# Sums of weight blocks moved from VectorE to GpSimd, with planning steps, loads and copies reordered and matmuls put between two stages

## Chip, cores, metric

One of the cores of a Trainium2 chip runs the whole program. The metric is the device time of one execution in microseconds; lower is better.

## What is computed

x is 32 batches of 64 rows and 1024 columns. Four layers are applied, each added to its input:

```python
# W0, W1: (16, 64, 64), picked per batch by itok_B_0_15
x = x + einsum('bct,bcd->bdt', x, W0[c])
x = x + einsum('bct,bcd->bdt', x, W1[c])
# W: (1024, 1024); lora_A: (5, 1024, 32); lora_B_w: (1024, 32)
x = x + einsum('bsi,oi->bso', x, W) + einsum('bsr,or->bso', einsum('bsi,bir->bsr', x, A[l]), B) * 0.5
# weight: (8, 1024, 1024), picked per batch by itok_B_3_7
x = x + einsum('bsi,boi->bso', x, weight[a])
```

## The kernel before

The two small layers act on the 64 rows and the two large ones on the 1024 columns, so the kernel does the large ones first on x transposed and applies the product of the two small ones (`mix_tab`, 16 matrices of 64x64) at the end. To each large weight the identity is added on its diagonal (`w_eyes`, L451; `A11`, L1088; `adapter_eyes`, L421), which gives the residual.

**Precision.** Every float32 operand is split into a high part (a copy to float32r by ACT: `w_hi`, `x_hi`) and a low part (source minus high part, by DVE: `w_lo`, `x_lo`). A product is then three matmuls, high by high, high by low, low by high (L1288 to L1290, in `main`). The semaphores `w_hi`, `x_hi`, `w_lo`, `x_lo` count tiles, four to a block.

**Layer 3 (W) as seven products.** W and x are cut in 2x2 blocks and multiplied by a Strassen scheme: seven weight blocks (w 0 to 6) and sixteen x blocks (x 0 to 15, twice seven and two), in two column groups j = 0 and 1. Some operands are sums of raw blocks. For the weights: S2 = `kw + w1t - w2t`, in `kw`; S3 = `w2t - w1t`, in `w2t`; S1 = w5's block + S2; S4 = w6's block - S2. For x: T1 to T4. Before, DVE forms all of them: `s2_and_s3` (L892, L894, L896), `s1` (L902), `s4` (L908), `t1` to `t4`. Each works on 128 partitions by 2048 columns.

**The low-rank part** is `low_rank(c, ...)` (L1315, 32 matmuls of 256 columns), done four times: the second one, `low_rank(1, 1, 3)`, waits for `x_lo` to reach 16, which is all of x block 3; the third, `low_rank(2, 11, 12)`, for all of x12. ACT and DVE then fold the result (`low_out`: L550, L555; `low_parts`: L922, L926), and a matmul adds it (L1327).

**Layer 4** is done slot by slot (two batches with the same adapter at a time; L1402, and L1429 for the mix with `mix_tab`). Which batches share a slot is worked out on the chip by `plan_steps`, a chain of about a hundred small DVE operations on 32 partitions, each waiting for the one before. It is a generator that yields after every few operations; `take(n)` emits the next n pieces at a place in DVE's order where there is room: `take(2)` ahead of `s2_and_s3`, `take(4)`, and a last `take()` with all the rest.

**Order.** Nothing is scheduled by a planner: each engine runs its instructions in the order in which its block is written, and waits on semaphores. The SP queue issues nearly all loads, in its own order, with waits of its own. PE starts with `warm(WARM)` (20 matmuls on zeroes), makes `mix_tab` (16 products of 64 columns, L1267, after DVE has made `w1_s` and `w0_twice` at L822 and L826), and goes on to the first product of layer 3.

Of the kernel before, what the change touches and what calls it, by code (L numbers as in the profile page):

```python
# [13 lines left out]
P = 128  # L14
# [14 lines left out]
RING = 12  # L29
UNIT = 2 * D  # L30
HALF = KT // 2
WARM = 20


BATCH0, BATCH1, SINGLE = (0, 5), (5, 5), (10, 1)
# [31 lines left out]
def build(nc, xt, indices, w0t, w1, wt, lora_a, lora_b, w3t, plan_c, eye_c, out):  # L67
# [120 lines left out]
    def s(name):  # L188
        if name not in sem:
            sem[name] = nc.alloc_semaphore(name)  # L190
        return sem[name]
# [56 lines left out]
    with nc.Block() as block:  # L248
# [3 lines left out]
        def _(sp):  # L252
# [5 lines left out]
            def load_x(n, half, c):  # L258
                if n >= 3:
                    wait_l2(sp, x_last[n - 3])  # L260
                sp.dma_start(raw_of(x_slot(n)), x_block(half, c)).then_inc(s(f"x_in{n}"), 16)

            def load_w(w, out_half, in_half):
                if w >= 3:
                    wait_l2(sp, w_last[w_before(w)])
                sp.dma_start(raw_of(w_slot(w)), w_block(out_half, in_half)).then_inc(s(f"w_in{w}"), 16)

            def load_stg(half, c):
                sp.dma_start(stg, x_block(half, c)).then_inc(s("stg"), 16)
# [39 lines left out]
            load_stg(1, 0)  # L309
            load_w(5, 1, 1)  # L310
            load_x(10, 1, 2)
            load_x(11, 1, 2)
            sp.wait_ge(s("T1"), 1)
            load_stg(2, 2)
            load_w(6, 1, 2)
            sp.wait_ge(s("S4"), 1)
            load_kw(x_block(1, 3))
# [91 lines left out]
        def _(pool):  # L409
# [38 lines left out]
            def w_eyes(dst, name):  # L448
                for k in range(HALF):
                    v = dst[:, k, P * k:P * (k + 1)]  # L450
                    pool.tensor_tensor(v, v, eye[:, 0:P], ALU.add).then_inc(s(name), 1)  # L451

            pool.wait_ge(s("S3"), 1)
            w_eyes(w2t, "S3")
            pool.wait_ge(s("w_in4"), 16)
            w_eyes(raw_of(w_slot(4)), "A22")
            pool.wait_ge(s("S1"), 1)
            w_eyes(raw_of(w_slot(5)), "S1")


            pool.wait_ge(s("low_lo"), 2 * CH)
# [39 lines left out]
        def _(act):  # L501
# [25 lines left out]
            def x_from(n, src, name, value):  # L527
                act.wait_ge(s(name), value)
                if src is not None:

                    wait_l2(act, x_last[n - 3])
                for ks in halves:
                    x_hi(n, raw_of(x_slot(n)) if src is None else src, ks)
# [36 lines left out]
            def c21(j, os=range(HALF)):  # L570

                act.wait_ge(s("seed"), HALF * (j + 1))
                copy_out("C21", 1, j, out_block(2, j), "c21", os)
# [9 lines left out]
            def w_from(w, src, name, value):  # L583
                act.wait_ge(s(name), value)
                if w >= 3 and src is not None:

                    wait_l2(act, w_last[w_before(w)])
                for ks in halves:
                    w_hi(w, raw_of(w_slot(w)) if src is None else src, ks)
# [43 lines left out]
            x_from(5, keep, "T3", 1)  # L633
            c11(1, last_two)
            w_from(3, w2t, "S3", HALF + 1)
            u2(0)
            x_from(6, None, "T4", 1)
            w_from(4, None, "A22", HALF)
            u3(0, first_two)
            for pair in range(8, 12):  # L640
# [7 lines left out]
            c21(0, last_two)  # L648

            act.wait_ge(s("x_lo"), HALF * 9)  # L650
            u2(1)
            x_from(9, None, "T4", 2)
            u3(1)
            w_from(5, None, "S1", HALF + 1)
            x_from(10, None, "T1", 1)
            c21(1, first_two)
            x_loaded(11)
            c21(1, (2,))
            x_from(12, stg, "stg", in_stg("B22_0"))
            c21(1, (3,))  # L660
            w_from(6, None, "S4", 1)
            low_out(2)
            for pair in range(12, 16):
                select(pair)
            x_from(13, kw, "T1", 2)
# [150 lines left out]
        def _(dve):  # L816
# [4 lines left out]
            v = w1_s.rearrange("p (c n) -> p c n", n=T)  # L821
            dve.tensor_tensor(v, v, eye[:, P:P + T].unsqueeze(1).to_broadcast([P, half, T]), ALU.add).then_inc(s("w01i"), 1)  # L822
            dve.wait_ge(s("w0"), 16)
            v = w0_s.rearrange("p (c n) -> p c n", n=T)
            for cs in (slice(0, half // 2), slice(half // 2, half)):
                dve.tensor_tensor(w0_twice[:, cs], v[:, cs].unsqueeze(2).to_broadcast([P, half // 2, 2, T]),  # L826
                                  eye[:, P:P + T].unsqueeze(1).unsqueeze(1).to_broadcast([P, half // 2, 2, T]), ALU.add)\
                   .then_inc(s("w01i"), 1)

            def w_lo(w, src, ks=slice(0, HALF)):  # L830
                dve.wait_ge(s("w_hi"), HALF * w + ks.stop)
# [13 lines left out]
            def w_los(w, src):  # L845
                for ks in halves:
                    w_lo(w, src, ks)

            def x_los(n, src=None):
                for ks in halves:  # L850
                    x_lo(n, src, ks)
# [24 lines left out]
            def t1(j):  # L876

                dve.wait_ge(s("stg"), in_stg(f"B11_{j} again"))
                if j == 0:
                    dve.wait_ge(s("x_in10"), 16)  # L880
                    v = raw_of(x_slot(10))
                else:
                    dve.wait_ge(s("kw"), 48)
                    v = kw
                dve.tensor_tensor(v, v, stg, ALU.subtract).then_inc(s("T1"), 1)

            def s2_and_s3():

                dve.wait_ge(s("w1t"), 16)
                dve.wait_ge(s("w2t"), 16)  # L890
                dve.wait_ge(s("kw"), 32)
                dve.tensor_tensor(kw, kw, w1t, ALU.add).then_inc(s("S2"), 1)  # L892
                dve.wait_ge(s("S2"), 1)
                dve.tensor_tensor(kw, kw, w2t, ALU.subtract).then_inc(s("S2"), 1)  # L894
                dve.wait_ge(s("S2"), 2)
                dve.tensor_tensor(w2t, w2t, w1t, ALU.subtract).then_inc(s("S3"), 1)  # L896

            def s1():

                dve.wait_ge(s("w_in5"), 16)  # L900
                v = raw_of(w_slot(5))
                dve.tensor_tensor(v, v, kw, ALU.add).then_inc(s("S1"), 1)  # L902

            def s4():

                dve.wait_ge(s("w_in6"), 16)
                v = raw_of(w_slot(6))
                dve.tensor_tensor(v, v, kw, ALU.subtract).then_inc(s("S4"), 1)  # L908

            def add_out(event, phase, j, src, dst, name, os=range(HALF)):  # L910
                for o in os:
# [166 lines left out]
            def take(n=None):  # L1078
                for _ in itertools.islice(making, n):
                    pass  # L1080
# [24 lines left out]
                                         ALU.mult, ALU.subtract).then_inc(s("b_split"), 1)  # L1105
            low_parts(0)
            dve.wait_ge(s("consts"), 32)
            take(2)
            s2_and_s3()
            x_los(3)  # L1110
            t3(0)
            t2(0)
# [2 lines left out]
            x_los(4, stg)  # L1115
            x_los(5, keep)
            w_los(3, w2t)
            take(4)
            t4(0)
            x_los(6)  # L1120
            w_los(4, raw_of(w_slot(4)))
# [4 lines left out]
            take()  # L1126
            t4(1)
            x_los(9)
            s1()
            t1(0)  # L1130
            w_los(5, raw_of(w_slot(5)))
            x_los(10)
            x_los(11)
            x_los(12, stg)
            s4()
            low_parts(2)
            w_los(6, raw_of(w_slot(6)))
            c22(0)
# [114 lines left out]
        def _(pe):  # L1253
# [6 lines left out]

            warm(WARM)

            for c in range(NC_ // 2):
                pe.wait_ge(s("w01i"), 2 if c < NC_ // 4 else 3)
                for g in range(2):
                    rows = slice(g * T, (g + 1) * T)
                    last = pe.matmul(ps_low[:, g, T * c:T * (c + 1)],  # L1267
                                     w0_twice[rows, c, :, :].rearrange("p h n -> p (h n)"),
                                     w1_s[rows, T * c:T * (c + 1)], start=True, stop=True)
            last.then_inc(s("mm"), 2)  # L1270

            def place_free(phase, j, o):
                n = HALF * (2 * phase + j) + o - NB
# [252 lines left out]
```

## Time and profile before

| | us |
|---|---|
| median of 3 runs | 394.65 |
| lowest, highest | 394.63, 395.87 |
| the profiled execution | 395.87 |
| its span | 394.1 |
| PE busy | 377.9 (96%) |
| DVE busy | 268.9 (68%) |
| ACT busy | 231.2 (59%) |
| POOL busy | 123.2 (31%) |

The span is what lies between the first and the last instruction of the profile. Times in the rows count from its start. A row of the timeline merges neighbouring instructions of one line; x2 behind it says that there are two. In square brackets stands the idle time of the engine before it and what ended it.

### The profile page before, as it was taken

To read this page: it belongs to the slowest core of one execution; us is meant where nothing else is said; L and a number is where in the kernel's file an instruction comes from. 1 tells how busy PE (TensorE), PEld (TensorE's weight loads), DVE (VectorE), ACT (ScalarE), POOL (GpSimd) and SP (SyncE) were. 2 spreads that over 40 slices of the span, in tenths; PEclk is the share of its full clock that TensorE was granted. 3 is DMA by queue.
4 is the path that set the end of the run, shared out by engine and by line. 5 is a ranking of instruction groups with operands and counts; after the bars stand their busy time and mean duration, and the time that the engine had idled before them with its cause. 6 is when DMAs were issued, how large, how long until landed. Compare 5 with 4: busy or idle time off the path is not lost.

```text
span 394.1 us, 7604 instructions
## 1 busy us (share of the span) xinstructions
PE 377.9 (96%) x1736; PEld 313.9 (80%) x1736; DVE 268.9 (68%) x285; ACT 231.2 (59%) x307; POOL 123.2 (31%) x163
## 2 busy tenths in 40 slices
PE   7989999999999999999999999899999999999981
PEld 6868888888888888888888887688888888888860
DVE  4766947864864968547968439953699446899562
ACT  3697849396332866244484549554677358777361
POOL 0000430100003000024864427753257434377400
PEclk9998999999999999999999999999999999999996
DMA  7985902741338565506518224742276322871223
GB/s 224 397 310 197 337 0 59 264 151 62 106 137 294 210 237 200 169 36 214 177 50 260 58 55 127 262 124 55 56 241 211 93 53 60 264 220 52 57 57 88
DMA packets 24219, 61.37 MB, mean 156 GB/s; under 512 B 1938, under 2 KB 2066, under 8 KB 24146
## 3 DMA queue, kind: packets, MB, share of 16 engines
q1 hardware_dynamic: 23808, 60.30, 46.3%
q8 instruction: 28, 0.46, 0.5%
q14 instruction: 45, 0.37, 0.3%
q10 hardware_dynamic: 338, 0.24, 0.2%
HBM read 52.15 MB, written 8.39 MB: 154 GB/s over the span
## 4 chain that ended last, share of the span: by engine, by line
PE 93%; issue 2%; DVE 1%; DMA 1%; ACT 1%; SPq 0%; ACTq 0%; DVEq 0%
PE ps L1402 44%; PE ps L1288 13%; PE ps L1290 13%; PE ps L1289 13%; PE ps L1315 4%; PE ps L1429 4%; PE ps L1327 2%; DMA ring_f<-wt 1%; DVE stage L1238 0%; DVE stage L1179 0%; PE ps L1448 0%; ACT stage L708 0%; DVE aT L1216 0%; DVE ring L833 0%; ACT ring L510 0%
## 5 line engine op out<-in xcount | busy, mean ns | idle before, releaser
L1402 PE MATMUL ps<-ring,aT 128*128 x784 | 180.8, 389 | 0.0
L1402 PEld LDWEIGHTS ps<-ring,aT 128*128 128x128 f32 x784 | 147.0, 188 | 30.9 <-issue 0.6
L1288 PE MATMUL ps<-ring 128*128 128x512 f32 x224 | 87.3, 390 | 1.2 <-DVE ring L840 1.2
L1289 PE MATMUL ps<-ring 128*128 128x512 f32 x224 | 87.2, 389 | 0.0
L1290 PE MATMUL ps<-ring 128*128 128x512 f32 x224 | 87.2, 389 | 0.0
L429 POOL TENSOR_TENSOR aT<-xT,aT 128x512 fp32r<-128x512 f32 (+1 forms) x36 | 55.9, 1574 | 48.5 <-ACT aT L687 43.4
L1151 DVE TENSOR_TENSOR ring<-raw,ring 128x1024 f32 (+1 forms) x40 | 64.4, 1668 | 5.1 <-ACT ring L673 5.0
L696 ACT ACTIVATE aT<-ps 64x1024 fp32r<-64x1024 f32 x32 | 32.7, 1023 | 47.5 <-PE ps L1402 47.0
L1168 DVE TENSOR_TENSOR aT<-ps,aT 64x1024 fp32r<-64x1024 f32 x32 | 39.1, 1222 | 22.6 <-ACT aT L696 21.9
L1179 DVE TENSOR_TENSOR stage<-ps,stage 64x1024 f32<-64x1024 f32 x30 | 36.7, 1222 | 26.0 <-ACT stage L708 25.3
L1288 PEld LDWEIGHTS ps<-ring 128*128 128x128 f32 x224 | 42.1, 188 | 9.9 <-DVE ring L833 1.3
L1290 PEld LDWEIGHTS ps<-ring 128*128 128x128 f32 x224 | 42.0, 188 | 8.7
L1289 PEld LDWEIGHTS ps<-ring 128*128 128x128 f32 x224 | 42.1, 188 | 8.6
L708 ACT ACTIVATE stage<-ps 64x1024 f32<-64x1024 f32 x30 | 30.6, 1018 | 23.8 <-PE ps L1429 23.4
L673 ACT ACTIVATE ring<-raw 128x1024 f32 (+1 forms) x40 | 39.6, 1049 | 8.0 <-POOL raw L421 5.6
L562 ACT ACTIVATE xT<-ps 128x512 f32<-128x512 f32 x40 | 22.6, 591 | 21.9 <-PE ps L1290 20.7
L421 POOL TENSOR_TENSOR raw<-raw,eye 128x128 f32<-128x128 f32 x40 | 20.6, 525 | 27.3 <-DMA raw<-w3t 23.2
L451 POOL TENSOR_TENSOR ring_f<-ring_f,eye 128x128 f32<-128x128 f32 x8 | 5.5, 718 | 68.9 <-DVE ring_f L902 50.6
L840 DVE TENSOR_TENSOR ring<-ring_f,ring 128x1024 fp32r<-128x1024 f32 (+1 forms) x20 | 21.9, 1127 | 5.6 <-ACT ring L513 5.5
L443 POOL CAST st<-aT 128x64 fp32r x34 | 19.1, 562 | 10.2 <-POOL st L445 7.6
L687 ACT ACTIVATE aT<-xT 128x512 fp32r (+1 forms) x36 | 19.9, 602 | 3.1 <-DVE xT L913 2.7
L451 POOL TENSOR_TENSOR xT<-xT,eye 128x128 f32<-128x128 f32 x4 | 7.7, 1942 | 43.7 <-DVE xT L896 43.7
(82 smaller groups left out, 312.0 us busy)
## 6 DMA issues: line engine op xcount, KB each, us to landing
raw<-w3t SPq DMA_DIRECT2D x40, 512.0 KB, 4.4
ring_f<-xt SPq DMA_DIRECT2D x8, 1024.0 KB, 8.2
raw<-xt SPq DMA_DIRECT2D x8, 1024.0 KB, 5.1
out<-stage SPq DMA_DIRECT2D x30, 256.0 KB, 3.0
ring_f<-wt SPq DMA_DIRECT2D x4, 1024.0 KB, 7.3
xT<-xt SPq DMA_DIRECT2D x3, 1024.0 KB, 9.5
xT<-wt SPq DMA_DIRECT2D x2, 1024.0 KB, 14.8
ring_f<-wt SPq DMA_DIRECT2D x4, 256.0 KB, 5.6
```

What stands on the lines that cost most here:

```text
L429: pool.tensor_tensor(x3_split(i, ks, P + h * T, T), xT[:, ks, bass.ds(which[h] * T, T)], as_f32(x3_split(i, ks, h * T, T)), ALU.subtract). ...
L562: act.activation(dst[:, o, :], ps_l2(phase, j, o), ACT.Copy).then_inc(s(name), 1)
L673: act.activation(dst, adapter_raw(t), ACT.Copy).then_inc(s("w_hi"), 1)
L696: act.activation(r_tile(h)[own, :], acc(i)[own, :, :].rearrange("p a n -> p (a n)"), ACT.Copy)\
L708: act.activation(stage[own, i % 2, :], mixed_ps[h][other, :, :].rearrange("p a n -> p (a n)"), ACT.Copy)\
L1151: dve.tensor_tensor(in_two(unit_of(t, 1)), adapter_raw(t), as_f32(in_two(unit_of(t, 0))), ALU.subtract)\
L1168: dve.tensor_tensor(r_tile(h)[other, :], acc(i)[own, :, :].rearrange("p a n -> p (a n)"), as_f32(r_tile(h)[own, :]), ALU.subtract).then_in ...
L1179: dve.tensor_tensor(dst, mixed_ps[h][own, :, :].rearrange("p a n -> p (a n)"), dst, ALU.add)\
L1288: pe.matmul(dst, hi_of(qw)[:, k, cs], hi_of(qx)[:, k, :], start=start and k == 0, stop=False, skip_group_check=True)
L1289: pe.matmul(dst, hi_of(qw)[:, k, cs], lo_of(qx)[:, k, :], start=False, stop=False, skip_group_check=True)
L1290: last = pe.matmul(dst, lo_of(qw)[:, k, cs], hi_of(qx)[:, k, :], start=False, stop=stop and k == HALF - 1, skip_group_check=True)
L1402: last = pe.matmul(acc(i)[:, n, :], x3_split(i, k, start, P), ring[:, bass.ds(off + (part * D + n * 512), 512)], start=(k == 0 and j == 0) ...
```

## The change

- **PE**: `mix_tab`'s sixteen products run over all eight column blocks of one half of the partitions and then of the other, and wait once; 20 more matmuls on zeroes (`BRIDGE`) stand between them and the first product of layer 3.
- **DVE**: `w0_twice` in one operation of 1024 columns instead of two; S2, S3, S1 and S4 leave DVE; `take(7)` instead of `take(2)` ahead of x block 3, and `take(2)` instead of `take(4)` ahead of T4; x10 is split ahead of w5.
- **POOL**: forms S2, S3, S1 and S4, each ahead of the diagonal that goes on it.
- **ACT**: x6 and x9 are copied one tile of `u2` earlier; x10 ahead of w5; `low_out(2)` ahead of w6.
- **SP**: the load of x11 stands behind the wait for T1 and the load of B22_0 to `stg`.

```diff
-WARM = 20
+WARM, BRIDGE = 20, 20
...
-            load_x(11, 1, 2)
             sp.wait_ge(s("T1"), 1)
             load_stg(2, 2)
+            load_x(11, 1, 2)
...
+            pool.wait_ge(s("w1t"), 16)
+            pool.wait_ge(s("w2t"), 16)
+            pool.wait_ge(s("kw"), 32)
+            pool.tensor_tensor(kw, kw, w1t, ALU.add).then_inc(s("S2"), 1)
+            pool.wait_ge(s("S2"), 1)
+            pool.tensor_tensor(kw, kw, w2t, ALU.subtract).then_inc(s("S2"), 1)
+            pool.wait_ge(s("S2"), 2)
+            pool.tensor_tensor(w2t, w2t, w1t, ALU.subtract).then_inc(s("S3"), 1)
             pool.wait_ge(s("S3"), 1)
             w_eyes(w2t, "S3")
             pool.wait_ge(s("w_in4"), 16)
             w_eyes(raw_of(w_slot(4)), "A22")
+
+            pool.wait_ge(s("w_in5"), 16)
+            v = raw_of(w_slot(5))
+            pool.tensor_tensor(v, v, kw, ALU.add).then_inc(s("S1"), 1)
             pool.wait_ge(s("S1"), 1)
-            w_eyes(raw_of(w_slot(5)), "S1")
+            w_eyes(v, "S1")
+            pool.wait_ge(s("w_in6"), 16)
+            v = raw_of(w_slot(6))
+            pool.tensor_tensor(v, v, kw, ALU.subtract).then_inc(s("S4"), 1)
...
-            u2(0)
+            u2(0, first_two)
+            u2(0, (2,))
             x_from(6, None, "T4", 1)
+            u2(0, (3,))
...
-            u2(1)
+            u2(1, first_two)
+            u2(1, (2,))
             x_from(9, None, "T4", 2)
+            u2(1, (3,))
             u3(1)
+            x_from(10, None, "T1", 1)
             w_from(5, None, "S1", HALF + 1)
-            x_from(10, None, "T1", 1)
...
+            low_out(2)
             w_from(6, None, "S4", 1)
-            low_out(2)
...
-            for cs in (slice(0, half // 2), slice(half // 2, half)):
-                dve.tensor_tensor(w0_twice[:, cs], ...).then_inc(s("w01i"), 1)
+            dve.tensor_tensor(w0_twice, ...).then_inc(s("w01i"), 1)
...
-            take(2)
-            s2_and_s3()
+            take(7)
             x_los(3)
...
-            take(4)
+            take(2)
             t4(0)
...
-            s1()
             t1(0)
+            x_los(10)
             w_los(5, raw_of(w_slot(5)))
-            x_los(10)
             x_los(11)
             x_los(12, stg)
-            s4()
...
-            for c in range(NC_ // 2):
-                pe.wait_ge(s("w01i"), 2 if c < NC_ // 4 else 3)
-                for g in range(2):
+            pe.wait_ge(s("w01i"), 2)
+            for g in range(2):
+                for c in range(NC_ // 2):
                     last = pe.matmul(...)
-            last.then_inc(s("mm"), 2)
+                last.then_inc(s("mm"), 1)
+            warm(BRIDGE)
```

DVE before, from the first planning steps to T3: `cells` holds the planning's values, `raw` is `kw` (or `stg`), `xT` holds `w1t`, `w2t` and `keep`.

```order
L963 CAST cells<-asked 32x32 [waits chain,consts]
L947 TENSOR_TENSOR cells<-cells,eye 32x32 [waits chain]
L959 TENSOR_REDUCE cells<-cells 32x1 [waits chain]
L947 TENSOR_TENSOR cells<-cells 32x256 [waits chain]
L959 TENSOR_REDUCE cells<-cells 32x8 [waits chain]
L892 TENSOR_TENSOR raw<-raw,xT 128x2048 [waits kw,w2t,w1t]
L894 TENSOR_TENSOR raw<-raw,xT 128x2048 [waits S2]
L896 TENSOR_TENSOR xT<-xT 128x4x512 [waits S2]
L840 TENSOR_TENSOR ring<-ring_f,ring 128x1024 [waits x_hi] x2
L857 TENSOR_TENSOR xT<-xT,raw 128x4x512 [waits stg,keep]
```

DVE in the change, the end of the same stretch (lines of the changed kernel, in which L858 is the split of x that was L840, and L875 is T3); ahead of these rows stand the same five planning steps and 15 more rows of planning:

```order
L958 COPY cells<-cells 32x32 [waits chain]
L962 STREAM_TRANSPOSE cells<-cells 32x32 [waits chain]
L950 SCALAR_TENSOR_TENSOR cells<-cells 32x32 [waits chain]
L954 TENSOR_REDUCE cells<-cells 32x1 [waits chain]
L950 SCALAR_TENSOR_TENSOR cells<-cells 32x32 [waits chain]
L954 TENSOR_REDUCE cells<-cells 32x1 [waits chain]
L946 TENSOR_SCALAR cells<-cells 32x32 [waits chain]
L954 TENSOR_REDUCE cells<-cells 32x1 [waits chain]
L858 TENSOR_TENSOR ring<-ring_f,ring 128x1024 [waits x_hi] x2
L875 TENSOR_TENSOR xT<-xT,raw 128x4x512 [waits stg,keep]
```

The three operations on 2048 columns are gone from here, and 25 planning operations have taken their place ahead of the split.

POOL before, between the first and the second clearing of `st`:

```order
L410 MEMSET st 128x512
L451 ISA
L451 TENSOR_TENSOR xT<-xT,eye 128x128 [waits S3,eye,zeroed]
L451 TENSOR_TENSOR xT<-xT,eye 128x128 x3
L451 TENSOR_TENSOR ring_f<-ring_f,eye 128x128 [waits w_in4]
L451 TENSOR_TENSOR ring_f<-ring_f,eye 128x128 x3
L451 TENSOR_TENSOR ring_f<-ring_f,eye 128x128 [waits S1]
L451 TENSOR_TENSOR ring_f<-ring_f,eye 128x128 x3
L463 MEMSET st 128x512 [waits low_hi,low_lo]
```

POOL in the change, the same stretch without its first two and its last row:

```order
L457 TENSOR_TENSOR raw<-raw,xT 128x2048 [waits w2t,w1t,kw,eye,zeroed]
L459 TENSOR_TENSOR raw<-raw,xT 128x2048 [waits S2]
L461 TENSOR_TENSOR xT<-xT 128x4x512 [waits S2]
L451 TENSOR_TENSOR xT<-xT,eye 128x128 [waits S3]
L451 TENSOR_TENSOR xT<-xT,eye 128x128 x3
L451 TENSOR_TENSOR ring_f<-ring_f,eye 128x128 [waits w_in4]
L451 TENSOR_TENSOR ring_f<-ring_f,eye 128x128 x3
L469 TENSOR_TENSOR ring_f<-ring_f,raw 128x2048 [waits w_in5]
L451 TENSOR_TENSOR ring_f<-ring_f,eye 128x128 [waits S1]
L451 TENSOR_TENSOR ring_f<-ring_f,eye 128x128 x3
L474 TENSOR_TENSOR ring_f<-ring_f,raw 128x2048 [waits w_in6]
```

Five operations on 2048 columns have come, the first three one behind the other.

ACT before, around w6 and `low_out(2)`; the last row of L513 is x12, L510 the two halves of w6:

```order
L513 ACTIVATE ring<-raw 128x1024 [waits l2,stg]
L513 ACTIVATE ring<-raw 128x1024
L562 ACTIVATE xT<-ps 128x512 [waits l2,seed]
L510 ACTIVATE ring<-ring_f 128x1024 [waits S4]
L510 ACTIVATE ring<-ring_f 128x1024
L550 ACTIVATE low<-ps 128x512 [waits l2]
L555 ACTIVATE low_split<-low 64x4x64 [waits l2,low_sum]
```

In the change the two rows of L510 stand behind all of `low_out(2)` (L550 and five of L555).

## Rows read from the trace of the kernel before

**Rows 1.** The page, busy time of the engines

```profile
PE 377.9 (96%) x1736; PEld 313.9 (80%) x1736; DVE 268.9 (68%) x285; ACT 231.2 (59%) x307; POOL 123.2 (31%) x163
```

**Rows 2.** PE's waits: who waited for whom, us in total, times, longest

```profile
PE ps L1448 <- DVE aT L1216: 3.3, 1, 3.3
PE ps L1315 <- issue: 2.0, 1, 2.0
```

**Rows 3.** The chain that ended last, in order of time: start, us, what

```profile
25.37 1.97 issue
27.34 5.55 PE ps L1315 x32
...
50.15 3.83 PE ps L1315 x32
...
138.33 3.83 PE ps L1315 x32
```

**Rows 4.** PE by stretch: length, PE busy (count), granted clock, DMA share, GB/s

```profile
27.00:28.00 1.00, 0.66 (x5) 1.00 0.46 170
28.00:29.00 1.00, 1.00 (x9) 0.70 0.09 35
29.00:30.00 1.00, 1.00 (x6) 0.50 0.00 0
```

**Rows 5.** DVE's timeline, 34 to 48 us: start, us, engine line operation

```profile
35.63 0.17 DVE L963 CAST cells<-asked 32x32 f32<-32x32 int32 x1
...
37.91 2.29 DVE L892 TENSOR_TENSOR raw<-raw,xT 128x2048 f32<-128x2048 f32 x1 [0.79 <-DMA raw<-wt]
...
44.77 2.62 DVE L840 TENSOR_TENSOR ring<-ring_f,ring 128x1024 fp32r<-128x1024 f32 x2
```

**Rows 6.** DVE's timeline, planning operations at 70 and 101 us

```profile
70.49 0.35 DVE L951 TENSOR_SCALAR cells<-cells 32x8 int32<-32x8 f32 x2
...
75.21 0.20 DVE L967 STREAM_TRANSPOSE cells<-cells 32x32 f32<-32x32 f32 x1
...
100.58 0.23 DVE L955 SCALAR_TENSOR_TENSOR cells<-cells 32x32 f32<-32x32 f32 x1
...
102.30 0.17 DVE L959 TENSOR_REDUCE cells<-cells 32x1 f32<-32x32 f32 x1
```

**Rows 7.** Timeline of POOL and DVE, single operations at 203 and 71 us

```profile
203.03 1.30 POOL L429 TENSOR_TENSOR aT<-xT,aT 128x512 fp32r<-128x512 f32 x1 [0.82 <-POOL st L445]
203.05 2.36 DVE L1151 TENSOR_TENSOR ring<-raw,ring 128x1024 f32 x1 [0.84 <-ACT ring L673]
204.28 2.28 POOL L429 TENSOR_TENSOR aT<-xT,aT 128x512 fp32r<-128x512 f32 x1
71.07 0.38 DVE L951 TENSOR_SCALAR cells<-cells 32x8 f32<-32x8 f32 x1
```

**Rows 8.** POOL's timeline, operations with nothing of DVE in the way

```profile
70.97 0.46 POOL L451 TENSOR_TENSOR ring_f<-ring_f,eye 128x128 f32<-128x128 f32 x1 [18.30 <-DMA ring_f<-wt]
216.78 2.55 POOL L429 TENSOR_TENSOR aT<-xT,aT 128x512 fp32r<-128x512 f32 x2 [1.29 <-issue]
```

**Rows 9.** Timeline of PE and DVE, 1 to 9 us

```profile
1.35 4.03 PE L1259 MATMUL ps<-st 128*128 128x256 f32 x20 [1.35 <-POOL st L410]
...
4.79 1.29 DVE L826 TENSOR_TENSOR stage<-stage,eye 128x512 f32<-128x512 f32 x2
...
5.54 2.00 PE L1267 MATMUL ps<-stage 64*128 64x64 f32 x32 [0.16 <-DVE stage L826]
...
8.77 0.47 PE L1288 MATMUL ps<-ring 128*128 128x512 f32 x1 [1.23 <-DVE ring L840]
```

**Rows 10.** Timeline of DVE, ACT and PE, 135 to 149 us

```profile
135.46 2.36 DVE L840 TENSOR_TENSOR ring<-raw,ring 128x1024 fp32r<-128x1024 f32 x2
140.11 2.01 ACT L510 ACTIVATE ring<-ring_f 128x1024 fp32r<-128x1024 f32 x2 [3.32 <-DVE ring_f L908]
143.55 2.18 ACT L555 ACTIVATE low_split<-low 64x256 fp32r<-64x256 f32 x5 [0.76 <-DVE low L922]
147.18 0.68 DVE L913 TENSOR_TENSOR xT<-ps,xT 128x512 f32<-128x512 f32 x1
148.37 0.39 PE L1288 MATMUL ps<-ring 128*128 128x512 f32 x1
```

More of the change, by code:

```diff
@@ L823, in _ @@
             dve.wait_ge(s("w0"), 16)
-            v = w0_s.rearrange("p (c n) -> p c n", n=T)
-            for cs in (slice(0, half // 2), slice(half // 2, half)):
-                dve.tensor_tensor(w0_twice[:, cs], v[:, cs].unsqueeze(2).to_broadcast([P, half // 2, 2, T]),
-                                  eye[:, P:P + T].unsqueeze(1).unsqueeze(1).to_broadcast([P, half // 2, 2, T]), ALU.add)\
-                   .then_inc(s("w01i"), 1)
+            dve.tensor_tensor(w0_twice, w0_s.rearrange("p (c n) -> p c n", n=T).unsqueeze(2).to_broadcast([P, half, 2, T]),
+                              eye[:, P:P + T].unsqueeze(1).unsqueeze(1).to_broadcast([P, half, 2, T]), ALU.add)\
+               .then_inc(s("w01i"), 1)
             def w_lo(w, src, ks=slice(0, HALF)):
@@ L885, in t1 @@
                 dve.tensor_tensor(v, v, stg, ALU.subtract).then_inc(s("T1"), 1)
[L887 to L908, printed above, removed]
             def add_out(event, phase, j, src, dst, name, os=range(HALF)):
@@ L1261, in _ @@
             warm(WARM)
-            for c in range(NC_ // 2):
-                pe.wait_ge(s("w01i"), 2 if c < NC_ // 4 else 3)
-                for g in range(2):
-                    rows = slice(g * T, (g + 1) * T)
+            pe.wait_ge(s("w01i"), 2)
+            for g in range(2):
+                rows = slice(g * T, (g + 1) * T)
+                for c in range(NC_ // 2):
                     last = pe.matmul(ps_low[:, g, T * c:T * (c + 1)],
```

## The prediction

> **What bounds the kernel now.** I read the page's list of busy time first: TensorE (PE) is at work for 377.9 of the 394.1 us [rows 1], so only what stops it or slows its clock counts. The list of PE's waits comes second [rows 2]: the one at the tail (3.3 us, before L1448) is not touched by the change; the one of 2.0 us before L1315, the first low-rank product, is. The chain in order of time [rows 3] places it: PE stops at 25.37, starts L1315 at 27.34, takes 5.55 us for its 32 matmuls, and from there shows no idle time up to the second low-rank product at 50.15, where the same 32 matmuls take 3.83. The difference, 1.7 us, is the clock: the granted clock stands at 0.50 of full, 1.2 instead of 2.4 GHz, from about 28.3 to 31.6, after the stop [rows 4]. The third low-rank product starts at 138.33 [rows 3]. The gain within reach at the front is therefore 2.0 + 1.7 us; what can be lost is whatever VectorE (DVE), ScalarE (ACT) or GpSimd (POOL) delivers late. The second low-rank product waits for all four low tiles of x block 3 (`x_lo` 16); DVE makes them in the two L840 that end at 47.39 [rows 5], 2.8 us before PE wants them at 50.15.
>
> **The front of PE.** w0_twice in one step ends at the same time as both halves did (4.79 + 1.29 = 6.08), so the sixteen small products start at 6.1 rather than 5.54 [rows 9]. They took 2.0 us; twenty bridge matmuls of 256 columns follow, at 0.12 us each (3.83 / 32, rows 3) 2.4 us. The main products start at 6.1 + 2.0 + 2.4 = 10.5 instead of 8.77: 1.7 late. From both sides: if the small products, now all of one half of the rows before the other, take twice as long (4.0) and the bridge runs like the warm-up (4.03), 14.1, that is 5.3 late. Taking the first, because the warm-up has ended its slow part by then, the 1.97 us stop shrinks to 0.2, L1315 starts at 27.3 as before, at full clock, and PE is ready for the second low-rank product at 50.15 - 1.7 = 48.4.
>
> **S2 and S3 move to POOL, and planning steps move ahead of x block 3.** This is the term that decides. On DVE, before: five planning operations from 35.63, three operations of 2.29 us from 37.91 (when `kw` has landed), then the split of x block 3 from 44.77 [rows 5]. After: thirty planning operations, then the split; the three big ones run on POOL meanwhile.
>
> Alone, the 25 added operations cost about what left: 19 of them ran from 70.49 to 75.41 and six from 100.58 to 102.47 [rows 6], together 4.9 + 1.9 = 6.8 us against 6.9. What changes the sum is that POOL and DVE hold each other up. At 203 us [rows 7] POOL's first L429 takes 1.30, the DVE operation issued beside it takes 2.36 where two of that size take 2.36 together elsewhere [rows 10], and POOL's next takes 2.28: each waits for the whole of the other's operation and then they take turns. It holds for the small planning operations as well: the first one beside a POOL operation of 0.46 takes 0.38 [rows 7], where two took 0.35 just before [rows 6]. The Trainium skill (SBUF — State Buffer, "SBUF: two separate sides") says the port pair that the two share is locked for a whole instruction; the trace agrees up to 512 columns, and no row has a longer POOL operation. By a lock let go within it, the rival below applies.
>
> Price of one POOL operation on 2048 columns: 0.46 us for 128 columns, 2.55 / 2 = 1.27 for 512 [rows 8], so 2.1 ns a column, and 0.46 + 1920 x 2.1 ns = 4.5 us. The upper bound is 4 x 1.27 = 5.1, the lower 2048 x 2.1 ns = 4.3, without a cost to start; I take 4.5. The Trainium skill (GPSIMD Engine Reference, "Elementwise — side-by-side cycle accounting") gives 4497 ns for this very operation; by it the sum is the same.
>
> - POOL starts at 37.9. Three operations, with a semaphore wait or a turn of DVE (0.2) between them: 3 x 4.5 + 0.4, done at 51.8.
> - DVE's chain of planning steps has some 4 to 8 of its 25 added operations done by 37.9. Between two POOL operations it gets a turn of one or two that read two tiles, plus a reduction: some four operations in all. At 51.8, 13 to 17 are left: 2.7 to 3.5 us at 0.2 each, plus 0.8 because the four diagonal additions (L451) take turns with them. Done at 55.3 to 56.1.
> - The split of x block 3, twice 1.18: ready at 57.7 to 58.5; I take 58.1, and PE starts 0.1 later, as it did after the stop at 25.37. With 5.1 per POOL operation it is 60.
>
> PE, ready at 48.4, stands still for almost 10 us. Against before, the second low-rank product starts at 58.2 instead of 50.15: **+8.1 us**. The gain of the bridge is inside that: whatever PE saves before 48.4 is spent waiting. After such a stop the clock is down when PE comes back. It cost 1.7 us the first time; I take **+1.7** again, with 1.0 and 3.3 (the whole slow stretch lasting twice as long) as bounds. What is next late then is nothing: T3, T2 and the rest of DVE's list follow x block 3 directly, and PE is as far behind as they are.
>
> **The middle.** The later planning steps get 3 to 4 us shorter each time, and DVE no longer has S1; x6 and x9 are split one copy earlier by ACT. All of this feeds products before which PE shows no wait, so it is worth nothing by itself. S1 on POOL (4.5 instead of 2.29, and a turn against T1) is covered by those same microseconds and by the split of x10, now ahead of w5. `load_x(11)` now waits for T1; T1 comes earlier by more than 2 us for want of S1, and PE needs x11 and x12 only at 138.33.
>
> **S4, x12 and low_out(2).** (Times on the old clock, leaving the shift aside.) S4 on POOL takes 4.5 us and may take its turn ahead of the split of x12, which DVE ended at 135.46 + 2.36 = 137.8 [rows 10], 0.5 before PE's 138.33. DVE arrives some 2.3 us earlier (no S1), so the excess is between 0 and 4.5 - 2.8 = 1.7; I take **+0.5**. After it, w6 is split behind low_out(2) on ACT: its copies end at 143.55 + 2.18 = 145.73 and then L510 takes 2.01, where before it ran at 140.11, in ACT's gap [rows 10]. DVE's second half of w6 follows to 149.0, the first c22 tile (0.68, in DVE's order behind w6) to 149.7; it was done at 147.86 and PE used it at 148.37. **+1.3**; bounds 0 (if low_out comes first by more) and 1.4.
>
> **The sum.** 8.1 + 1.7 + 0.5 + 1.3 = 11.6 us. The profiled run took 395.87, its span 394.1, so 1.77 lie outside the span; 395.87 + 11.6 = 407.5. The median of the three is 394.65, the profiled one the highest, by 1.2; I leave my number at the profiled run, since PE's start after x block 3 depends on DVE and POOL and not on where that 1.2 lay, and let the range take it in.
>
> **Rivals.**
> 1. *POOL does not hold DVE through a 2048-column operation* (it lets go within, or planning steps slip through). If nothing is held, planning ends at about 42, x block 3 is ready near 45 and PE never waits there: -1.7 for the clock, +1.3 for c22: 395.5, or 394.2 from the median: no change. Without the c22 wait too, 393.0: faster by 0.4%. Rows 7 speak against it; for it speaks only that they show nothing longer than 512 columns. The point that decides: it is right if DVE's two-input operations stay at their plain durations between 38 and 52.
> 2. *It lets go in pieces of 512 columns or so*: each of about 12 planning operations waits some 1.2 us, x block 3 is ready at 53 to 56: 402 to 405, inside my range.
> 3. *The bridge is long* (5.3 late): PE would come at 51.8 to the second low-rank product. In my case that is covered by the 58.1. In rival 1 it adds 3.3 and ends at 397.6 to 398.8: slower.
> 4. *POOL dearer* (5.1 us, and the slow clock twice as long): +1.9 and +1.6, with 1.7 for x12 instead of 0.5: 412.
>
> **How the numbers follow.** My case 0.78 (404 to 411), rival 2 0.05, rival 4 0.05, rival 3 in rival 1 0.02, rival 1 0.10, shared evenly between no change and faster. About 0.3% (1.2 us) is what can be told from no change here. Faster 0.05, same 0.05, slower 0.90. The range goes from 401 (rival 2 from the median) to 412.5.
>
> **What would show it.** Right: PE idle for 8 to 11 us before its second low-rank product, released by DVE's split of x block 3; three POOL operations of about 4.5 us from 38 to 52, with single planning operations of DVE stretched to over 4 us beside them; no stop at 25.4; the granted clock at 0.5 shortly after 58; about 1 us of idle before the first of w6's products. Wrong: POOL's three end later than 55 or are chopped up, or DVE's planning operations run at 0.2 us beside them.

## The result, and where the time went

| | before | changed |
|---|---|---|
| median, us | 394.64 | 413.99 |
| lowest to highest | 394.57 to 395.87 | 413.89 to 414.06 |
| ratio (95% interval) | | 1.0482 (1.0461 to 1.0503) |
| profiled execution, its span | 395.87, 394.1 | 414.62, 412.9 |

The change makes the kernel 19.3 us slower. The forecast of slower holds; its size does not: 407.5 with a range up to 412.5 against 414.0.

PE's waits in the changed kernel (who waited for whom, us in total, times, longest), which answer to [rows 2]. Lines are those of the changed kernel: L1308 is the low-rank product that was L1315, L1281 the first matmul of a split product, L858 the split of an x block, L908 the addition that makes a c22 tile.

```profile
PE ps L1308 <- issue: 8.4, 1, 8.4
PE ps L1308 <- DVE ring L858: 3.8, 1, 3.8
...
PE ps L1281 <- DVE xT L908: 1.4, 1, 1.4
```

Three new stops have come, and the one of 2.0 us of [rows 2] has gone. The chain in order of time (start, us, what) places the four low-rank products; before, they started at 27.34, 50.15, 138.33 [rows 3] and 165.76:

```profile
30.06 3.83 PE ps L1308 x32
...
59.52 6.31 PE ps L1308 x32
...
153.96 5.33 PE ps L1308 x32
...
184.58 3.83 PE ps L1308 x32
```

The lag against the kernel before is 2.7, 9.4, 15.6 and 18.8 us, and 18.8 at the end of the span. So nothing is lost behind 185 us. The 18.8 us split as 9.4 up to the second product, 2.5 inside it (6.31 instead of 3.83), 3.8 on the way to the third, 1.5 inside that (5.33), and 1.7 from there to the fourth (25.3 us instead of 23.6), of which the stop before w6's first product is 1.4. (Each part is rounded.)

The second product's 6.31 us are the clock, as [rows 4] showed it for a shorter stop. PE by stretch (length, busy and count, granted clock, DMA share, GB/s): PE is idle for 8.4 us from 51.1. The granted clock falls to half (1.2 GHz) inside that stop, at about 54.4, and stays there until about 64.6.

```profile
52.00:54.00 2.00, 0.00 (x0) 1.00 0.00 0
54.00:56.00 2.00, 0.00 (x0) 0.60 0.00 0
...
60.00:62.00 2.00, 2.00 (x11) 0.50 0.00 0
62.00:64.00 2.00, 2.00 (x11) 0.50 0.00 0
64.00:66.00 2.00, 2.00 (x15) 0.84 0.00 0
```

What PE waits for there stands in the timelines of POOL and DVE of the changed kernel (start, us, engine line operation), the counterparts of [rows 5]:

```profile
38.65 4.62 POOL L457 TENSOR_TENSOR raw<-raw,xT 128x2048 f32<-128x2048 f32 x1 [37.35 <-DMA raw<-wt]
43.35 4.64 POOL L459 TENSOR_TENSOR raw<-raw,xT 128x2048 f32<-128x2048 f32 x1
48.07 4.57 POOL L461 TENSOR_TENSOR xT<-xT 128x2048 f32<-128x2048 f32 x1
```

```profile
38.73 4.56 DVE L946 TENSOR_SCALAR cells<-cells 32x8 f32<-32x8 f32 x1
43.33 0.15 DVE L950 SCALAR_TENSOR_TENSOR cells<-cells 32x8 f32<-32x8 f32 x1
43.52 9.20 DVE L942 TENSOR_TENSOR cells<-cells 32x64 f32<-32x64 f32 x2
...
57.08 2.34 DVE L858 TENSOR_TENSOR ring<-ring_f,ring 128x1024 fp32r<-128x1024 f32 x2
```

A planning operation on 32 x 8 numbers takes 4.56 us, as long as the POOL operation beside it. The next one falls into the gap between two POOL operations and takes 0.15. The two behind it take 9.20 together, 4.55 and 4.61: each waits for a whole POOL operation. From 38.73 to 52.72 DVE gets four planning operations done, where it needs 0.2 us for each.

The stop before the third product, same columns. POOL's S4 (L474) takes its turn between the halves of x12 (the L858 that reads `raw`), so these two take 6.65 us instead of the 2.36 of [rows 10]:

```profile
144.68 2.36 DVE L858 TENSOR_TENSOR ring<-ring_f,ring 128x1024 fp32r<-128x1024 f32 x2 [3.08 <-ACT ring L529]
147.05 6.65 DVE L858 TENSOR_TENSOR ring<-raw,ring 128x1024 fp32r<-128x1024 f32 x2
```

```profile
146.16 5.33 POOL L474 TENSOR_TENSOR ring_f<-ring_f,raw 128x2048 f32<-128x2048 f32 x1 [9.04 <-DMA ring_f<-wt]
```

That the halves of x12 did not come earlier has its cause further up, in T1 and in the load of x11 behind it. T1 before (L885) and after (L903), and beside it S1 on POOL:

```profile
123.80 2.52 DVE L885 TENSOR_TENSOR ring_f<-ring_f,raw 128x2048 f32<-128x2048 f32 x1 [0.59 <-DMA ring_f<-xt]
```

```profile
131.40 4.13 DVE L903 TENSOR_TENSOR ring_f<-ring_f,raw 128x2048 f32<-128x2048 f32 x1 [7.83 <-DMA ring_f<-xt]
128.76 4.61 POOL L469 TENSOR_TENSOR ring_f<-ring_f,raw 128x2048 f32<-128x2048 f32 x1 [44.24 <-DMA ring_f<-wt]
```

The load of x11, as SP issues it. Before, it is the second of two in one row, issued at 121.13; after, it stands alone:

```profile
114.02 7.48 SPq L261 DMA_DIRECT2D ring_f<-xt  x2
```

```profile
135.97 0.51 SPq L261 DMA_DIRECT2D ring_f<-xt  x1
```

T1's data has landed at 131.40, but S1 runs on POOL until 133.37, and T1 takes 4.13 us instead of 2.52. The load of x11 waits for its end.

### The profile page after: what moved, and what is told of

It reads as the page before. It is cut to its first block, busy times and chain, and to the rows that moved or that the text cites. A ratio compares the mean times of both kernels' runs of the same rounds, so it can differ in the third digit from the quotient of the medians.

```text
span 412.9 us, 7643 instructions
## 1 busy us (share of the span) xinstructions
PE 386.6 (94%) x1756; PEld 322.0 (78%) x1756; DVE 275.8 (67%) x279; ACT 231.1 (56%) x307; POOL 140.9 (34%) x168
## 4 chain that ended last, share of the span: by engine, by line
PE 84%; issue 5%; DMA 4%; DVE 4%; ACT 1%; ACTq 0%; SPq 0%; POOL 0%; DVEq 0%; POOLq 0%
PE ps L1395 42%; PE ps L1281 10%; PE ps L1283 10%; PE ps L1282 10%; PE ps L1308 5%; DMA ring_f<-xt 4%; PE ps L1422 4%; PE ps L1251 2%; PE ps L1320 1%; DVE ring L858 1%; DVE ring_f L903 1%; PE ps L1259 1%; DVE ring L851 0%; DVE stage L1230 0%; DVE stage L1171 0%
## 5 line engine op out<-in xcount | busy, mean ns | idle before, releaser
L1281 PE MATMUL ps<-ring 128*128 128x512 f32 x224 | 87.4, 390 | 1.4 <-DVE xT L908 1.4
L1171 DVE TENSOR_TENSOR stage<-ps,stage 64x1024 f32<-64x1024 f32 x30 | 36.7, 1222 | 26.0 <-ACT stage L728 25.3
L1281 PEld LDWEIGHTS ps<-ring 128*128 128x128 f32 x224 | 42.1, 188 | 10.4 <-DVE xT L908 1.8
L1308 PE MATMUL ps<-ring,a_sel 128*128 128x256 f32 x128 | 19.6, 322 | 12.2 <-issue 8.4
L1308 PEld LDWEIGHTS ps<-ring,a_sel 128*128 128x128 f32 x128 | 19.2, 232 | 13.1 <-issue 12.9
L421 POOL TENSOR_TENSOR raw<-raw,eye 128x128 f32<-128x128 f32 x40 | 19.1, 488 | 27.7 <-DMA raw<-w3t 24.8
L858 DVE TENSOR_TENSOR ring<-ring_f,ring 128x1024 fp32r<-128x1024 f32 (+1 forms) x20 | 21.8, 1122 | 9.8 <-ACT ring L529 9.8
L529 ACT ACTIVATE ring<-ring_f 128x1024 fp32r<-128x1024 f32 (+1 forms) x20 | 18.5, 964 | 6.5 <-DMA ring_f<-xt 3.0
```

The costliest lines, as they stand in the source:

```text
L1171: dve.tensor_tensor(dst, mixed_ps[h][own, :, :].rearrange("p a n -> p (a n)"), dst, ALU.add)\
L1281: pe.matmul(dst, hi_of(qw)[:, k, cs], hi_of(qx)[:, k, :], start=start and k == 0, stop=False, skip_group_check=True)
L1308: last = pe.matmul(ps_low[:, j // 2, 2 * P * (j % 2):2 * P * (j % 2 + 1)], a_sel[:, pair % SEL, k, :, :, :].rearrange("p h t r -> p (h t r)"),
```

## Experiments

Three theories of the loss were put to the test. **L**: DVE and POOL take turns by whole instructions, and this makes x block 3 and x12 late. **P**: the planning operations ahead of x block 3 make it late by their number. **D**: the late load of x11 takes the slack. Runs named a_ start from the changed kernel, those named b_ from the kernel before. In the three groups of runs the kernel before had medians of 394.8, 394.8 and 395.2.

### S2 and S3 alone, on POOL (b_s23_pool)

```diff
 # in DVE's order
-            s2_and_s3()
 # in POOL's order, ahead of w_eyes(w2t, "S3")
+            pool.tensor_tensor(kw, kw, w1t, ALU.add).then_inc(s("S2"), 1)
+            ...
```

> The kernel before with S2 and S3 on POOL instead of DVE and nothing else: five planning operations, then the split of x block 3. Theory L: its two halves take turns with POOL's three operations (4.6 us each), x block 3 is ready near 54 instead of 47.4, PE stops 5 to 6 us before the second low-rank product, which then runs 1.5 to 2 us long on a slow clock: 400 to 401. If moving the planning steps were needed for the loss: 394.8.

Measured: 401.54 (ratio 1.0164, 1.0131 to 1.0197). DVE's timeline: the two halves of x block 3 (L848 here), free to start at 43.2, take 10.77 us where they took 2.62 [rows 5].

```profile
43.22 10.77 DVE L848 TENSOR_TENSOR ring<-ring_f,ring 128x1024 fp32r<-128x1024 f32 x2 [6.77 <-ACT ring L521]
```

The chain has the second low-rank product 3.9 us late (50.15 before) and slow. It also has the stop of 2.0 us before the first one, as the kernel before does [rows 3], but here that product takes 4.07 and not 5.55, and the granted clock stays at 1.00 from 24 to 34 us:

```profile
25.44 2.00 issue
27.43 4.07 PE ps L1311 x32
...
54.09 5.63 PE ps L1311 x32
```

So the move of three operations to another engine costs a third of the loss by itself, with no planning step moved. L holds; moving the planning steps is not needed for this loss. And the 1.7 us of slow clock at the front are a matter of the execution: the same stop of 2.0 us did not bring them here.

### S2 and S3 back on DVE, all planning steps ahead (a_s23_dve)

```diff
-            take(7)
+            take(2)
+            (S2 and S3, three dve.tensor_tensor)
+            take(5)
             x_los(3)
```

> The changed kernel with S2 and S3 back on DVE (after the first five planning operations), all thirty planning operations still ahead of x block 3. Theory L (turns: each DVE operation on two tiles waits for a whole POOL operation of 4.6 us): the planning operations take 0.15 to 0.25 us each again, x block 3 is ready near 53, PE stops some 2 us before the second low-rank product instead of 8.4, and the time is about 407. Theory P (the planning operations are what is late, whatever POOL does): their number ahead of x block 3 is the same, so the time stays at 414.

Measured: 408.6 (1.035, 1.0299 to 1.0401), 1.6 above what L said and 5.4 below P. The planning operations are short again; DVE reaches x block 3 at 51.85 and PE's second low-rank product starts at 54.29:

```profile
45.53 0.35 DVE L938 TENSOR_SCALAR cells<-cells 32x8 int32<-32x8 f32 x2
...
51.85 2.34 DVE L850 TENSOR_TENSOR ring<-ring_f,ring 128x1024 fp32r<-128x1024 f32 x2
```

### Planning steps moved back (a_take2, a_front_old)

```diff
 # a_take2; a_front_old also has S2 and S3 on DVE, between the two
-            take(7)
+            take(2)
             x_los(3)
 ...
-            take(2)
+            take(7)
             t4(0)
```

> The changed kernel with only five planning operations ahead of x block 3 (the other 25 ahead of T4), S2 and S3 still on POOL. Theory L: the two halves of the split of x block 3 each wait for a POOL operation, so it is ready near 54 and PE still stops for some 3 to 4 us: about 409. Theory P: x block 3 is ready near 47, PE does not stop at the second low-rank product, its clock stays up: 414 - 8.4 - 2.5 = 403.

Measured: 413.15 (1.0469, 1.0412 to 1.0526).

> The changed kernel with both undone: S2 and S3 on DVE, five planning operations ahead of x block 3. Both theories: no stop before the second low-rank product and no slow clock there, 403. It measures what the front costs in all, and leaves the bridge, S1 and S4 on POOL, the load of x11 and the order of w6: 403 - 394.6 = 8.4 should be left to them, of which about 1 for the bridge and small products.

Measured: 409.85 (1.0385, 1.035 to 1.0419).

Both missed by 4 and 7 us, and the front is not where. For it L's numbers are right: the second low-rank product starts at 54.90 in a_take2 (59.52 in the changed kernel) and, with its two halves of x block 3 stretched to 9.25 us, not at 51 as P has it; in a_front_old it starts at 52.40 and runs at full clock.

```profile
45.55 9.25 DVE L858 TENSOR_TENSOR ring<-ring_f,ring 128x1024 fp32r<-128x1024 f32 x2 [7.41 <-ACT ring L529]
```

What was won there was given back by my own edit. It put all 25 planning steps ahead of T4. In a_front_old T4 starts at 81.23, 25.0 us behind the end of the second low-rank product; in the changed kernel these are 19.6, before the change 21.4. From there one chain of DVE and loads (T4, T3, T2, T4 again, the load of x10, T1, the load of x11, x12) runs at its own pace. S1 still lengthens T1 in it (3.97 and 4.05 us), and S4 still takes its turn of 4.5 us inside x12. PE waits at its end, 7.4 us in both:

```profile
PE ps L1308 <- DVE ring L858: 7.4, 1, 7.4
```

That chain has half a microsecond of slack before the change [rows 10]. That is why what was won at the front in these two did not reach the end: from the end of the second product to the start of the third they take 92.2 us, the changed kernel 88.1, the kernel before 84.3.

### The load of x11 (a_x11, b_x11)

```diff
 # a_x11; b_x11 is the reverse on the kernel before
+            load_x(11, 1, 2)
             sp.wait_ge(s("T1"), 1)
             load_stg(2, 2)
-            load_x(11, 1, 2)
```

> The changed kernel with the load of x11 back ahead of the wait for T1. Theory D (the late load of x11 took the slack that would have covered the wait for S4 on POOL): ACT does not wait for x11, w6 lands some 2.6 us earlier, S4 is through earlier and x12 is ready near 150.5 instead of 153.7; with the clock kept up 409. Theory L alone (only the turn that S4 takes ahead of x12 matters, whenever w6 lands): x12 waits as long as before and the time stays within 1 us of 414.

Measured: 410.09 (1.0392, 1.0358 to 1.0425). The third low-rank product starts 84.8 us behind the end of the second, where it was 88.1 in the changed kernel and 84.3 before. S4 on POOL now runs ahead of x12 from 143.39, and x12's first half still waits for it (4.41 us for the two), but from an earlier time:

```profile
146.00 4.41 DVE L858 TENSOR_TENSOR ring<-raw,ring 128x1024 fp32r<-128x1024 f32 x2 [2.29 <-ACT ring L529]
```

> The kernel before with the load of x11 behind the wait for T1 and nothing else. Theory D (its wait moves x11 onto the path, with 0.5 us of slack left): x11 lands near 134, two us after ACT is ready for it, x12 is ready near 140.2 and the third low-rank product starts some 2 us late, on a slow clock if the stop is long enough: 396.8 to 398.5. If T1 alone with S1 off DVE decides: 394.8.

Measured: 396.7 (1.0052, 1.0022 to 1.0082). PE's waits show the stop before the third product that D expects:

```profile
PE ps L1315 <- DVE ring L840: 2.1, 1, 2.1
```

The load alone costs 1.5 us of the median, and the time is just below the 396.8 to 398.5 that D gave. The two causes share one slack: with the load early, the turn of S4 costs a stop of 0.5 us; with the load late and no S4 on POOL (next run), there is no stop at all.

### S4 back on DVE (a_s4_dve)

```diff
 # in POOL's order
-            pool.tensor_tensor(v, v, kw, ALU.subtract).then_inc(s("S4"), 1)
 # in DVE's order
             x_los(12, stg)
+            dve.tensor_tensor(v, v, kw, ALU.subtract).then_inc(s("S4"), 1)
             low_parts(2)
```

> The changed kernel with S4 back on DVE, behind the split of x12 as before the change; the load of x11 stays late. Theory L (S4 on POOL takes its turn between the two halves of x12 and holds the second for 4.3 us): x12 is ready 4 us earlier, PE does not stop before the third low-rank product (3.8 us) and its clock stays up there (1.5 us): about 409. Theory D (the late load of x11 is what makes x12 late): nothing changes, 414.

Measured: 408.89 (1.0346, 1.0312 to 1.0379), as L says. x12 takes its plain 2.36 us and the third low-rank product runs at full clock.

```profile
146.08 2.36 DVE L855 TENSOR_TENSOR ring<-raw,ring 128x1024 fp32r<-128x1024 f32 x2
148.36 2.29 DVE L1127 TENSOR_TENSOR ring_f<-ring_f,raw 128x2048 f32<-128x2048 f32 x1
```

The stop of 3.8 us and the slow clock behind it need both: either edit alone takes away 4 to 5 us.

### POOL's operations in four pieces (a_pieces)

```diff
-            pool.tensor_tensor(kw, kw, w1t, ALU.add).then_inc(s("S2"), 1)
+            for k in range(HALF):
+                pool.tensor_tensor(kw[:, k, :], kw[:, k, :], w1t[:, k, :], ALU.add).then_inc(s("S2p"), 1)
 # and so for the other two
```

> The changed kernel with each of S2's two operations and S3 cut into four operations of 512 columns on POOL. Theory L with whole instructions held: a planning operation waits 1.3 us at most instead of 4.6, but one after the other does, some twelve of them, and POOL's work gets longer by their turns, so x block 3 is ready at 57 to 59 as before and the time is 413 to 416. If a POOL operation let go inside itself, cutting it would change no duration of DVE's: the planning operations would still show 4.6.

Measured: 412.59 (1.044, 1.0405 to 1.0475). That is 0.4 below the lowest that L gave, and x block 3 is ready at 56.3 instead of 57 to 59. The planning operations that are held now take 0.9 to 1.24 us, at most the length of a piece, and not 4.6: each waits for one whole instruction of POOL, at 512 columns as at 2048.

```profile
41.66 1.22 DVE L949 TENSOR_SCALAR cells<-cells 32x8 f32<-32x8 f32 x1
42.92 1.24 DVE L953 SCALAR_TENSOR_TENSOR cells<-cells 32x32 f32<-32x32 f32 x1
44.20 0.17 DVE L957 TENSOR_REDUCE cells<-cells 32x1 f32<-32x32 f32 x1
...
46.79 1.23 DVE L961 COPY cells<-cells 32x32 f32<-32x32 f32 x1
48.06 0.20 DVE L965 STREAM_TRANSPOSE cells<-cells 32x32 f32<-32x32 f32 x1
```

### w6 ahead of low_out(2) (a_w6first)

```diff
-            low_out(2)
             w_from(6, None, "S4", 1)
+            low_out(2)
```

> The changed kernel with w6 copied ahead of low_out(2), as before the change. The third low-rank product starts late there, so S4 on POOL is through before it ends: the wait of 1.4 us for the first c22 tile goes, nothing else moves: 412.6. If it grows somewhere else (low_out held up by w6), 414.

Measured: 412.7 (1.0438, 1.0398 to 1.0479). The wait of PE before L1281 is gone from its list, and from the end of the third low-rank product to the start of the fourth PE takes 23.6 us, as before the change, where the changed kernel takes 25.3. So the order on ACT costs 1.7 us in the trace. The medians differ by 1.3, but this run's four times spread over 2.4, so they alone would not show it.

### The front of PE (b_bridge, b_serial)

```diff
 # b_bridge
             last.then_inc(s("mm"), 2)
+            warm(BRIDGE)
```

> The kernel before with 20 matmuls on zeroes behind the small products, nothing else. Theory G (they fill the stop before the first low-rank product, so the clock does not fall after it): the main products start 1.1 to 2.9 us later, the stop of 2.0 us shrinks or goes, the 1.7 us of slow clock go: 392.8 to 394. Theory N (PE idles elsewhere or the clock falls anyway): no gain, up to 1 us slower, 394.6 to 395.6.

Measured: 394.48 (0.9985, 0.9971 to 1.0), between what the two theories gave. The interval touches 1, so a gain of 0.3 us is likely and not certain. The twelve times lie between 394.06 and 395.13, those of the kernel before in the same group between 393.95 and 396.93. The bridge takes 2.66 us, the stop before the first low-rank product shrinks from 2.0 to 0.8, and that product takes 4.06 instead of 5.55:

```profile
27.61 4.06 PE ps L1316 x32
...
48.92 3.83 PE ps L1316 x32
```

The 5.55 are those of the one execution of [rows 3]; b_s23_pool has 4.07 behind a stop of 2.0. So most of the 1.7 us that G counts on is not there to be won in every execution, which fits a gain of 0.3.

```diff
 # b_serial
-            for c in range(NC_ // 2):
-                pe.wait_ge(s("w01i"), 2 if c < NC_ // 4 else 3)
-                for g in range(2):
+            pe.wait_ge(s("w01i"), 3)
+            for g in range(2):
+                for c in range(NC_ // 2):
```

> The kernel before with the sixteen small products run over one half of the partitions and then the other, and one wait. Theory R (neighbours on different halves overlap on PE, neighbours on the same half do not): they take 3.6 us instead of 2.0, end at 9.7 and push the main products back by 0.9 us, which the stop of 2.0 us before the first low-rank product takes in: no change of the time, 394.6. Theory C (they took 3.65 us in the changed kernel because its clock was down): they take 2.0 again.

Measured: 395.33 (1.0006, 0.9981 to 1.0031): no change of the time. The profiled execution took 397.83, 2.5 above that median. The small products take 6.30 us in it, worse than both theories, and the main products behind them start at 12.21, 0.42 us apart instead of 0.23:

```profile
5.98 6.30 PE L1267 MATMUL ps<-stage 64*128 64x64 f32 x32
12.21 0.79 PE L1288 MATMUL ps<-ring 128*128 128x512 f32 x1
12.80 0.63 PE L1289 MATMUL ps<-ring 128*128 128x512 f32 x1
13.22 0.63 PE L1290 MATMUL ps<-ring 128*128 128x512 f32 x1
```

In the changed kernel they took 3.69, and the granted clock is at half in its bridge: 4.15 us for 20 matmuls that took 2.66 in b_bridge:

```profile
11.00:12.00 1.00, 1.00 (x7) 0.50 1.04 404
```

The traces of all the runs tell the two apart. With the interleaved order the small products take 2.0 to 2.2 us, in four kernels; with the serial order 3.4 to 4.7 in nine and 6.30 in b_serial. In a_four they take 3.39 and the bridge right behind them 2.65, at full clock: the order costs some 1.4 us without a slow clock near it. The slow clock does not hang on the order. It is absent behind the serial order in a_four, and it is there behind the interleaved order in b_x11, where the main products lie 0.43 us apart from 9.73 to 11.86. Why b_serial's 6.30 are so much longer than the rest stays open. In the changed kernel PE is ready for the second low-rank product at 51.1 and waits until 59.5, so nearly all of this is covered by that stop.

### Four parts undone together (a_four)

S2, S3 and S4 on DVE, `take(2)` and `take(4)` where they stood, the load of x11 early; the other edits stay.

> The changed kernel with four parts undone: S2, S3 and S4 on DVE, the planning steps split as before, the load of x11 early. Left are the bridge and the order of the small products, S1 on POOL, and the orders on ACT. If the four make up the loss, what is left is 1.0 us at the second low-rank product and the 1.4 us wait for c22: 397. If they do not, it stays above 400.

Measured: 398.77 (1.0099, 1.0064 to 1.0133), 1.8 above what was expected. It is 15.2 below the changed kernel and 3.5 above the kernel before in the same group, so 15 to 16 of the 19.3 us are these four. The profiled execution took 397.06, below the median of its runs. There, the c22 wait of 1.4 is the largest stop that did not exist before. The other runs' 1.5 to 2.3 us more were not profiled; that they lie in the front, whose length varies with the clock in b_serial too, is a guess. S1 on POOL and the order of x6, x9 and x10 on ACT and DVE were not undone one by one: they are among what is left in this run, 3.5 us in all together with the bridge and c22.

## Why the prediction was right and wrong

By its own steps.

- **What bounds it; where PE stops.** Right. PE stops before the second low-rank product, released by x block 3, and nothing behind 185 us moves.
- **Turns by whole instructions.** Right, and the deciding step: b_s23_pool, a_pieces and a_s4_dve show it. By "SBUF: two separate sides" of the Trainium skill's page SBUF — State Buffer, the shared ports are locked for a whole instruction; the trace now agrees for POOL operations of up to 4.6 us.
- **The price of a POOL operation.** 4.5 forecast, 4.57 to 4.64 measured.
- **x block 3 ready at 58.1.** It was 59.4. POOL started 0.75 us later (38.65, because the load of `kw` was issued at 33.47 instead of 32.78), its three operations with their gaps took 14.0 instead of 13.9, and the planning rest with the four diagonal additions 0.5 more than taken. The count was near: 18 of the 25 added operations were left when POOL was through, where 13 to 17 were forecast, and four had got through beside POOL, as forecast. Term +8.1, measured +9.4.
- **The front of PE.** The sum took the short end, 10.5 for the start of the main products; it was 13.6, near the long end of 14.1. The reason I gave for the short end (the slow clock has ended) failed: the bridge ran at half clock. It cost nothing directly, since the main stop swallowed it. But in b_s23_pool, which has the old front, the load of `kw` is issued at 32.88, so some 0.6 of the 0.75 us above go with the later front. That ACT's copies, which release the load, were late behind PE is argued and not tested.
- **The clock behind the long stop.** +1.7 taken over from a stop of 2.0 us; 2.5 measured behind one of 8.4. The bound of 3.3 held it. The 1.7 were no price of a stop of 2.0 us, though: b_s23_pool has that stop without them. So the "gain within reach at the front" of 2.0 + 1.7 was that of one execution.
- **x12 and S4.** This is the step that failed: +0.5, bound 1.7; measured 3.8, and 1.5 more for the clock, a cost that the sum did not have. The mechanism was named rightly (S4 takes its turn ahead of x12). The size rested on "DVE arrives some 2.3 us earlier (no S1)". T1 did come 2.6 us earlier. (These times are on the old clock: 11.85 us, the lag at the end of the second low-rank product, are taken off.) But the load of x11 now starts behind it, at 124.1 instead of 121.1, ACT waits for it, and DVE splits x11 at 132.8 and x12 from 135.2, against 135.46 before. That is 0.3 us earlier and not 2.3, and S4's whole turn falls on PE but for the half microsecond of slack. The slack I counted twice, once for T1 and once for x12, was used up by the load. "T1 comes earlier by more than 2 us for want of S1, and PE needs x11 and x12 only at 138.33" set the load's cost at nothing without asking what its landing does to ACT's and DVE's order; a_x11 gives back 3.9 us and b_x11 shows 2.1 us of stop for it alone. S1's "turn against T1" was called covered, and that failed in the same way: T1 lies on the chain to x12 (T1, the load of x11, ACT's copy, the splits), and S1's turn makes it 1.6 us longer. What these 1.6 are worth in the end no run shows, since S1 alone was never put back.
- **c22 behind low_out(2).** +1.3 forecast; the stop is 1.4 and the whole stretch 1.7 longer, which a_w6first takes away.
- **The middle.** "Worth nothing by itself" holds for the gains; that there was slack for losses does not. The chain from T4 to x12 has 0.5 us, and a_take2 and a_front_old fell into it.

Together, in us, the five terms measured 1.3, 0.8, 3.3, 1.5 and 0.4 more than the sum had: 7.2 before rounding, on top of 11.6, which is the 18.8 of the spans. Of these, 4.8 are the step of x12 and S4 with the clock behind it. Without them the changed kernel would be at about 409.2 (an estimate: 413.99 - 4.8), inside the 404 to 411 of my case.

The rivals: the first (POOL does not hold DVE) is ruled out by the 4.56 us operation; the second (pieces of 512) by the same row, and a_pieces shows what it would have looked like. The third was true of the front and hidden. The fourth, at 412, was the nearest, for another reason: POOL was not dearer, but the slow clock and x12 were.

None of these versions beats both kernels clearly; the bridge alone on the kernel before, 394.48, is as good or 0.3 us better.

## What to carry to other kernels

Work moved from DVE to POOL still took DVE's time here. Each long POOL operation held one DVE operation for its whole length, so a chain of small dependent operations was the worst neighbour: four of them took 14 us. Shorter pieces only spread the wait (a_pieces is 1.4 us better). Before a load is put behind a wait, count not only when its data is used but what stands behind it in the order of the engine that reads it first. When several edits draw on one slack, sum them along the chain and spend the slack once. And a loss that was read in one execution, like the slow clock at the front, need not be in the others.

## What the runs showed of the hardware

- Which DVE operations are held: beside POOL's pieces in a_pieces a TENSOR_SCALAR with one input (1.22), a COPY of float32 (1.23), SCALAR_TENSOR_TENSOR (1.24) and TENSOR_TENSOR are; TENSOR_REDUCE (0.17) and STREAM_TRANSPOSE (0.20) are not. I had counted on the two-input ones mainly.
- What the slow clock costs behind a stop does not follow from the length of the stop. Behind 2.0 us it was 1.7 in the kernel before and nothing in b_s23_pool (4.07 us, granted clock 1.00). Behind longer stops a low-rank product took 1.5 more (3.8, changed kernel), 1.8 (5.3, b_s23_pool), 1.6 (7.4, a_front_old), 2.5 (8.4, changed kernel), and 2.8 behind only 3.5 (a_pieces).
- Sixteen small products on alternating halves of the partitions take 2.0 to 2.2 us, on one half after the other 3.4 to 4.7 in nine kernels and 6.3 in b_serial.
- In b_serial the granted clock is shown as 1.00 while matmuls are 0.42 us apart; the column can't be relied on in the first microseconds of that trace.
